# A fused attention and mixture-of-experts layer on one core: four small moves in the order of the work

## The reference

```python
Q, K = relu(x Wq + bq) * decay, relu(x Wk + bk) * decay;  V = x Wv + bv
out  = (Q @ (K^T V)) / (Q . sum(K) + 1e-6)          # linear attention, per head
x1   = layernorm(x + out Wo + bo)
gate = top_k(softmax(x1 @ w_gate), 2), normed
routed = sum over the two experts of gate_e * (silu(x1 G_e) * (x1 U_e)) @ D_e
shared = (silu(x1 G) * (x1 U)) @ D
y    = layernorm(x1 + routed + shared)
```

## Time and profile before

| | us |
|---|---|
| three executions | 241.12, 241.35, 244.77 (median 241.35) |
| the profiled execution | 242.8 |
| its span in the trace | 241.0 |
| PE busy | 221.6 (92% of the span) |
| DVE busy | 154.1 (64%) |
| POOL busy | 137.3 (57%) |
| ACT busy | 115.7 (48%) |

### The profile page before, as it was taken

The page is one execution under the profiler, slowest core; times in us unless marked ns, Lnnn a source line. Parts: engine busy times, 40 slices in busy tenths (PEclk is TensorE's granted clock), DMA queues, the critical chain, the costliest instruction groups (busy, mean ns, idle before and its releaser), DMA issues.

```text
span 241.0 us, 5038 instructions
## 1 busy us (share of the span) xinstructions
PE 221.6 (92%) x1440; PEld 193.9 (80%) x1440; DVE 154.1 (64%) x528; ACT 115.7 (48%) x298; POOL 137.3 (57%) x163
## 2 busy tenths in 40 slices
PE   8999999989899999979999789999999989999950
PEld 2478888879678888758899679999999978889940
DVE  2762373356767575964889776666666632799960
ACT  2282612761274361257206257778777853413450
POOL 0057689799768877747378006667767772003260
PEclk9999999999999999979999999999999999999995
DMA  6964572422312033002155225656665512961252
GB/s 158 363 218 104 152 252 84 122 62 81 87 47 88 25 110 111 22 33 101 44 184 171 71 84 163 187 171 172 184 175 174 160 53 46 383 196 75 91 176 85
DMA packets 21580, 31.72 MB, mean 132 GB/s; under 512 B 3248, under 2 KB 14257, under 8 KB 21556
## 3 DMA queue, kind: packets, MB, share of 16 engines
q1 hardware_dynamic: 17552, 22.46, 31.3%
q0 software_dynamic: 3456, 8.43, 10.0%
q10 hardware_dynamic: 548, 0.53, 0.8%
HBM read 19.70 MB, written 12.76 MB: 135 GB/s over the span
## 4 chain that ended last, share of the span: by engine, by line
PE 64%; DVE 19%; SPq 4%; issue 4%; ACT 3%; DMA 2%; POOL 1%; POOLq 0%; DVEq 0%
PE bank L335 12%; PE bank L337 12%; PE bank L336 11%; DVE x L1255 4%; PE bank L635 3%; PE bank L377 3%; PE bank L536 3%; PE bank L662 2%; PE bank L561 2%; DVE xt_raw L1064 2%; PE bank L455 2%; SPq L290 2%; PE bank L665 2%; PE bank L653 2%; PE bank L663 2%
## 5 line engine op out<-in xcount | busy, mean ns | idle before, releaser
L1408 POOL DMA_INDIRECT y_pairs<-x_t,dst x40 | 38.9, 973 | 29.5 <-DVE dst L1149 25.3
L1371 POOL DMA_INDIRECT x_slots<-x,slot x32 | 31.9, 996 | 16.5 <-issue 8.3
L335 PE MATMUL bank<-x1t_hi,wf_hi 128*128 128x512 f32 x64 | 26.7, 417 | 1.9 <-DVE xt_raw L1064 1.8
L337 PE MATMUL bank<-x1t_hi,wf_lo 128*128 128x512 f32 x64 | 26.0, 406 | 0.0
L336 PE MATMUL bank<-x1t_lo,wf_hi 128*128 128x512 f32 x64 | 25.8, 403 | 0.0
L335 PE MATMUL bank<-wf_hi,ot_hi 128*128 x80 | 25.7, 322 | 0.0
L1352 POOL TENSOR_TENSOR wf_lo<-stage,wf_hi 128x512 fp32r<-128x512 f32 x18 | 23.2, 1286 | 1.4
L337 PE MATMUL bank<-wf_hi,ot_lo 128*128 x80 | 22.6, 282 | 0.0
L336 PE MATMUL bank<-wf_lo,ot_hi 128*128 x80 | 22.4, 280 | 0.0
L749 ACT ACTIVATE k_sb<-bank,cst 128x256 f32<-128x256 f32 x16 | 7.7, 479 | 30.2 <-PE bank L352 28.5
L1149 DVE SCALAR_TENSOR_TENSOR dst<-o_sb,te_f 128x1 f32 (+1 forms) x40 | 8.8, 220 | 16.6 <-ACT ot_hi L863 16.5
(11 more groups left out here) (181 smaller groups left out, 693.5 us busy)
## 6 DMA issues: line engine op xcount, KB each, us to landing
o_sb<-x_slots SPq DMA_DIRECT2D x40, 129.0 KB
stage<-in_wffn SPq DMA_DIRECT2D x18, 256.0 KB, 2.8
x<-in_x SPq DMA_DIRECT2D x4, 512.0 KB, 7.0
out<-x SPq DMA_DIRECT2D x8, 256.0 KB, 2.1
xt_raw<-in_xT SPq DMA_DIRECT2D x3, 512.0 KB, 6.3
x_slots<-fill SPq DMA_DIRECT2D x9, 129.0 KB, 3.0
x<-in_watt SPq DMA_DIRECT2D x4, 256.0 KB, 6.3
k_sb<-y_pairs SPq DMA_DIRECT2D x2, 512.0 KB, 4.1
```

What stands on the lines that cost most here:

```text
L335: mm(o, w_hi, m_hi, start=start, stop=False, **more)
L337: return mm(o, w_lo, m_hi, start=False, stop=stop, **more)
L1371: pool.indirect_dma_start(out=x_scat, out_offset=bass.IndirectOffsetOnAxis(ap=slot[:, j, t:t + 1], axis=0), in_=x1[:, t, :], in_offset=Non ...
L1408: pool.indirect_dma_start(out=y_scat, out_offset=bass.IndirectOffsetOnAxis(ap=dst[:, j:j + 1], axis=0), in_=ey[:, u, :], in_offset=None, b ...
```

## The change

Four edits move work; no instruction is added or taken away.

1. On PE, `ranks(0)` stands behind the third projection tile of the next batch, no longer ahead of it (the same line holds for `b = 2` alone in this loop).
2. On POOL, `x1_lo(2)` goes ahead of `x1_norm(3)`, and `scatter(1, 1)` goes behind it.
3. On ACT and DVE, the first expert tile's Silu and product go ahead of the cast and the subtraction of shared chunk (2, 1).
4. On PE, shared chunk (2, 2) is computed in the last two steps of the expert loop: its gate half ahead of the transpose of `h` of tile 39, its up half ahead of the last down product.

```diff
                     attend(b, range(0, 2))
+                    proj_kv(b + 1, 2)
                     if b >= 2:
                         ranks(b - 2)
-                    proj_kv(b + 1, 2)
                     proj_kv(b + 1, 3)
...
                     e_gate_up(s + 1, (s + 1) % RING, expert[s + 1])
+                if s >= NT - 1:
+                    shared_gu(2, AHEAD, part=s - (NT - 1))
                 if s < NT:
                     e_h_transposed(s, s % RING)
                 expert.append(e_down(s - 1, (s - 1) % RING, expert[s - 1], s + 2 if s + 2 < NT else None))
...
-            for c in range(AHEAD, CS):
+            for c in range(AHEAD + 1, CS):
                 shared_gu(2, c)
...
             e_x_hi(2, 2)
+            e_silu(0, 0)
             shared_hh(2, 1)
-            e_silu(0, 0)
...
             e_x_lo(2, 2)
+            e_h(0, 0)
             shared_lo(2, 1)
-            e_h(0, 0)
...
             scatter(1, 0)
+            x1_lo(NB - 2)
+            x1_norm(3)
             scatter(1, 1)
-            x1_norm(3)
-            x1_lo(NB - 2)
             scatter(2, 0)
```

## The result

The changed kernel takes 239.55 us (median of 20 runs, 238.08 to 241.85), the kernel before, measured beside it, 242.27 us (20 runs, 240.14 to 245.11): ratio 0.9906, 95% interval 0.9883 to 0.9929. That is 2.3 us (1.7 to 2.8) faster where 4.95 were forecast, and 1.15 us above the top of the range. By the medians it is 2.7 us. By the border of 2% it is no change. The profiled execution took 238.08 us, its fastest, with a span of 236.3.

The account below looks back on a forecast made before the run. The prediction took PE, busy for 92% of the span, as the bound, with DVE at the end. Its terms 0.7 + 2.7 + 0.4 + 1.15 = 4.95 us, off 241.35, gave 236.4 us, with a range of 235.3 to 238.4.

Parts of the forecast that it names:

- Edit 1: Batch 0's ranks on PE: the 1.14 us wait for `hot_m` goes, 0.7 us gained, bounds 0 and 1.6.
- the slack that is gone: Between the end of ACT's apply and PE's transposes for batch 2: only 0.74 us fits in.
- the forecast wait at line 444: PE at batch 2's transposes: a new wait of about 0.9 us for ACT's apply.
- Edit 2: Batch 2's `top_two` and the PE work behind it: 2.7 us gained, bounds 1.6 and 3.0.
- the two blocked steps: Index cast and compares of batch 2's `top_two` on DVE, slowed by POOL's subtraction: 1.65 us net to win.
- a fall of the clock: PE clock at one half near 105 us, behind batch 2's ranks: expected gone with less idling, forecast 1.05 us.
- the clock gives nothing: Rival: the clock falls anyway, or timed executions before lack the fall; edit 2 gives 1.65, time 237.45; chance 0.20.
- the rival on the issues: Four scatter issues on POOL each block a small `top_two` step; edit 2 gives about 0.3, time 238.85; chance 0.10.
- Edit 3: First expert tile: PE's 1.13 us wait for its product shrinks, 0.4 us gained, bounds 0 and 0.9.
- Edit 4: Last two expert tiles: PE's idle 0.51 and 0.65 us filled, 1.15 us gained, bounds -0.35 and 1.45.
- the tail gives nothing: Rival: last send or landing is later, DVE waits at its first sums; sum 3.45, time 237.9; chance 0.11.

Follow-up runs that it names:

- the two quarters: Edits 1 to 3 plus only the gate half of shared chunk (2, 2), split in two across the last two expert steps, against before: 236.37 us, ratio 0.9827.

## Why the prediction was half right

**Edit 1, forecast 0.7.** Right as far as it can be told, in mechanism too: 0.6 us by the slack that is gone, 0.8 by the start of the transposes in 16 traces, 0.9 by its own median, whose interval reaches zero. The transposes now follow ACT's apply at once, and the forecast wait at line 444 is there in five of nine traces. Their start hangs on POOL's queue, which varies by 2 us. The wait of 1.14 us itself is not in every execution: in two of the seven traces without the edit PE waits 0.2 us or less for batch 0's ranks.

**Edit 2, forecast 2.7.** Right in sum, and in part by luck. The mechanism holds: the two blocked steps were worth 1.95 us (the column falls from 19.95 to 17.99), forecast 1.65, and a fall of the clock costs 1.45, forecast 1.05. That is 3.4 us up to chunk 1, above the bound of 3.0. What the prediction had wrong is that it took the fall for a property of the kernel; it is one of about half of its executions. So the rival "the clock gives nothing" is true for the other half, and the two errors offset each other: 1.95 and about 0.65 make 2.6, where the runs gave 2.5 to 2.9 with an interval from 1.2 to 3.9. Of the rival on the issues the mechanism is there, and its price was wrong: two copies are held up to the end of an issue, which costs the 0.2 us that the forecast charged (0.38 less 0.17), and not one small step after another.

**Edit 3, forecast 0.4.** Right at its place, 0.48 us by the traces. Whether it reaches the end stays open: its own runs show no gain (ratio 0.9994, 0.4% either way), and the tile loop behind it varies by six times as much.

**Edit 4, forecast 1.15.** This is the step that failed, and it failed at two sentences: the send "moves from 199.82, where POOL's own queue had held it, to about 200.15", and "So the pair loads start 0.35 us later". PE's part was right: the last down product came 1.16 us later where 1.1 was forecast, and DVE would have asked for its first load 1.6 us earlier (1.4 by the two quarters). But the loads started 2.64 us later against tile 38's `h`, not 0.35.

One part, 0.66 us, could have been read from the kernel before. Its last copy on ACT:

```profile
198.62 0.37 ACT L878 COPY x_t<-bank 128x256 f32<-128x256 f32 x1 [0.90 <-PE bank L665]
```

It ended at 198.99, and the send began at 199.82, 0.83 us behind. A send for which POOL waits begins 0.77 us behind the copy's end. So POOL's queue had held this send by 0.06 us, where the forecast needed 0.75 (1.1 less 0.35), and the send came 1.01 us later.

The other part, 1.63 us, was in no row of before: the instruction packet between the last send's packets. Four traces with the whole of edit 4 have both packet and delay (4.06 to 4.17), and all traces without the packet at that place have 2.45 or 2.46, one of them with POOL waiting. In all four the three late packets begin within 0.02 us of the instruction packet's end. That the packet causes the delay rests on these coincidences; it is not shown by moving the packet alone, since the attempt did not move it. And the late packets account for 0.9 of the 1.63 us; why the load is issued another 0.7 us later is open.

DVE's room ahead of the first load then decides: before, the load landed 2.0 us ahead of DVE's asking (the prediction looked at `v_sb` and had 1.6). Now DVE asks 1.6 us earlier (11.16 us behind tile 38's `h`, not 12.79) and the load lands 2.4 us later (13.16, not 10.76), so DVE waits 2.0 us; it waited 2.03, and its first sum began 0.4 to 0.6 us later than without edit 4. An estimate without the packet is 5.40 + 2.45 + 3.9 = 11.75 us from tile 38 to the first sum in place of 12.8: 1.05 us gained, close to the forecast even though the send is late. The rival "the tail gives nothing" named this place and its mechanism, and priced it at -0.35, where it is -0.5 by the traces and -0.5 to -1.6 by the runs.

**The sum.** 0.8 + 2.6 + 0.5 - 0.5 = 3.4 us by stages, against 2.3 (1.7 to 2.8) and 3.0 by the ratios of the two measurements of the changed kernel. The stages promise more than the runs give, so one of the terms is still too high; the clock (0.65) and edit 3 (0.5), which their own runs do not show at the end, are the likeliest, and that is not shown. The forecast time of 236.4 is 3.15 us too low: 1.65 of it is edit 4, 0.9 is the base (three runs gave 241.35 where 20 gave 242.27, and the time was counted from the former), and the last 0.6 stays open.

## What to carry to other kernels

Filling an engine's holes is safest with pieces that fit them: in holes of 0.5 and 0.65 us two pieces of 0.7 us gave 1.4 us up to the first sum and left the last send where it was, while two pieces of 1.4 us made that send 1.0 us late and gave nothing. A piece too large is not lost in itself (three quarters of the chunk gave 1.5 us); it uses up the room of the transfer behind it, and then anything else that delays the transfer, here a packet, reaches the end. Before work is put ahead of the last producer of a transfer, read how much room the landing has, and how long the issuing engine takes from its release to its start (0.77 us here): only what is left beyond that is slack of its queue. And cut the program into stages between fixed instructions over several traces: here two stages vary by 2 to 3 us, the rest by 0.1, and only in the latter can an edit of half a microsecond be seen.

## What the runs showed of the chip that I had not expected

Where an instruction packet of 0.02 MB began beside the packets of a send, 3 of those 48 came about 0.9 us late, when the packet had ended, and the load behind the send was issued 1.6 us later than otherwise. The packet keeps to a place in PE's program: in all twenty traces it comes when PE has 157 to 168 of its products left. Edit 4 puts twelve products ahead of the last down product, and so brings the packet from 5.6 to 6.4 us behind the last send (on the ordinary chips) to 1.65 to 1.7; the half chunk brings it to 2.8 or 2.9, which is far enough. Why it keeps to that place is open: 24 more instructions at PE's start moved the first such packet by some 4 us and this one not at all.

POOL's issue of an indirect DMA holds up copies and casts of DVE in its last half microsecond alone. Of the 105 of `top_two`'s casts and copies in the twenty traces that begin beside an issue of a `scatter`, the 37 that begin 0.27 to 0.48 us ahead of its end all end 0.02 to 0.03 us ahead of it and take 0.24 to 0.45 us; those that begin earlier take 0.16 to 0.20 us.

After the same idle time of PE, 1.75 us behind a shorter wait, the granted clock fell to 0.50 in three traces with the old order on POOL and stayed at 1.00 in two. By the mean clock of each run, an estimate, it falls in 33 of 72 executions of one and the same kernel.

On one of the chips used the same kernels took 11% longer, with PE standing in part without a cause that the trace names, and even there three quarters of the chunk were fastest and edit 2 with two quarters came next.
